# Attention and expert block: the first chunk's value products in key-tile order, with the wait for the fourth tile's copy moved ahead of its own products

## The reference, cut to what matters

```python
q, k, v = (einsum('bnd,fd->bnf', layernorm(x), W) for W in (Wq, Wk, Wv))   # heads of 64
sim = 50 * tanh(einsum('bhid,bhjd->bhij', q, k) * 64**-0.5 / 50)
attn = softmax(where(causal, sim, lowest))
x = x + einsum('bhij,bhjd->bhid', attn, v) @ Wo.T
x = x + shared_ffn(layernorm(x)) + top2_experts(layernorm(x))
```

## Time and profile before

| what | value |
|---|---|
| median of 3 runs | 2019.36 us (2017.86 to 2020.98) |
| profiled execution | 2022.81 us |
| its span from first to last instruction | 2021.0 us |
| TensorE matmul busy | 1915.1 us, 95% of the span |
| TensorE weight loads busy | 1496.6 us, 74% |
| VectorE busy | 1514.7 us, 75% |
| ScalarE busy | 1414.5 us, 70% |
| GpSimd busy | 1014.9 us, 50% |

### The profile page before, as it was taken

The page is one execution under the profiler, slowest core; times in us unless marked ns, Lnnn a source line. Parts: engine busy times, 40 slices in busy tenths (PEclk is TensorE's granted clock), DMA queues, the critical chain, the costliest instruction groups (busy, mean ns, idle before and its releaser), DMA issues. The chain is left out here.

```text
span 2021.0 us, 40088 instructions
## 1 busy us (share of the span) xinstructions
PE 1915.1 (95%) x14511; PEld 1496.6 (74%) x14511; DVE 1514.7 (75%) x2933; ACT 1414.5 (70%) x2169; POOL 1014.9 (50%) x1195
## 2 busy tenths in 40 slices
PE   6899999999999999999999999999999985998998
PEld 5676767676777777777777777777777754898998
DVE  5577777777878787878777777777777676677777
ACT  6878787878787777777777777777777752444444
POOL 4444555555555545454646464646454542444444
PEclk9999999999999999999999999999999996999999
DMA  4000000000000001010101010101010124665764
GB/s 136 1 12 10 32 22 32 22 33 22 27 27 22 32 17 38 12 43 12 43 12 43 12 43 12 43 12 43 11 43 1 43 74 152 211 189 175 207 196 132
DMA packets 74511, 113.56 MB, mean 56 GB/s; under 512 B 10441, under 2 KB 52942, under 8 KB 74192
## 3 DMA queue, kind: packets, MB, share of 16 engines
q1 hardware_dynamic: 59312, 68.90, 11.5%
q0 software_dynamic: 15008, 42.10, 5.5%
HBM read 64.13 MB, written 48.65 MB: 56 GB/s over the span
## 5 line engine op out<-in xcount | busy, mean ns | idle before, releaser
L523 POOL TENSOR_SCALAR_AFFINE_SELECT prob<-prob 128x256 f32<-128x256 f32 x512 | 222.7, 456 | 651.1 <-ACT prob L613 646.1
L607 ACT ACTIVATE prob<-ring 128x1024 f32<-128x1024 f32 (+1 forms) x384 | 324.1, 874 | 159.7 <-PE ring L1275 152.7
L613 ACT ACTIVATE prob<-prob 128x1024 f32<-128x1024 f32 (+1 forms) x384 | 346.6, 917 | 6.0
L808 DVE TENSOR_TENSOR kT<-ring,kT 64x512 fp32r<-64x512 f32 x256 | 176.3, 689 | 204.2 <-ACT kT L620 171.1
L1291 PE MATMUL bank_o<-prob,v 128*32 128x512 f32 (+3 forms) x4096 | 302.5, 435 | 18.1 <-issue 15.4
L535 POOL TENSOR_TENSOR key_sum<-prob 128x768 f32<-128x768 f32 x128 | 239.4, 1870 | 85.0 <-PE bank_d L1306 68.5
L1291 PEld LDWEIGHTS bank_o<-prob,v 128*32 128x32 f32 x4096 | 116.8, 109 | 184.9 <-issue 174.0
L1270 PE MATMUL ring<-qT,kT 128*128 128x256 f32 (+3 forms) x1024 | 239.9, 336 | 12.4 <-ACT qT L630 8.6
L1270 PEld LDWEIGHTS ring<-qT,kT 128*128 128x128 f32 x1024 | 162.9, 189 | 88.5 <-issue 39.5
L822 DVE RECIPROCAL norm<-bank_d 128x512 f32<-128x512 f32 x64 | 214.7, 3354 | 17.9 <-PE bank_d L1306 17.3
L1275 PE MATMUL ring<-q_lo,kT 128*128 128x256 f32 (+3 forms) x1024 | 227.0, 323 | 0.0
(11 more groups left out here) (222 smaller groups left out, 4654.9 us busy)
## 6 DMA issues: line engine op xcount, KB each, us to landing
xin<-first SPq DMA_DIRECT2D x71, 257.0 KB
xin<-second SPq DMA_DIRECT2D x71, 129.0 KB
xin<-base SPq DMA_DIRECT2D x71, 128.0 KB
x_next<-in_x SPq DMA_DIRECT2D x16, 512.0 KB, 3.9
x_res<-in_x SPq DMA_DIRECT2D x16, 512.0 KB, 3.9
raw_e<-in_w SPq DMA_DIRECT2D x4, 1024.0 KB, 6.6
first<-pad SPq DMA_DIRECT2D x9, 257.0 KB, 6.9
second<-pad SPq DMA_DIRECT2D x9, 129.0 KB, 6.5
```

The costliest lines, as they stand in the source:

```text
L523: last = nc.gpsimd.affine_select(out=diag, in_=diag, compare_op=ALU.is_ge, fill=0.0, base=0, pattern=[[0, 2], [1, P]], channel_multiplier=-1)
L607: nc.scalar.activation(probs[p % PROBS][u][:, :, :], slot[:, :, 0:UNIT_COLS[u]], ACT.Tanh, scale=SCALE / SOFTCLAMP).then_inc(act_emptied, 1)
L613: nc.scalar.activation(cols, cols, ACT.Exp, scale=SOFTCLAMP).then_inc(exp_done, 1)
L808: last = nc.vector.tensor_tensor(kT[head_rows[1 - h], h, :], slot[r, 1, :], kT[r, h, :].bitcast(F32), ALU.subtract)
```

## The change

In `values` the list of key tiles is sorted by key tile (0, 1, 2, 3 in place of 0, 1, 3, 2), in all 128 chunks. In chunk 0 of a sequence the wait ahead of the products is for the copy of `v`'s tile 2 (`NT - 2`) in place of tile 3, and the wait for tile 3's copy stands just ahead of the products of key tile 3. The sum over key tiles is the same, taken in another order.

```diff
--- before.py
+++ after.py
@@ -1281,11 +1281,13 @@
                 g, quad, half = i * PAIRS + c, c // 2, c % 2
                 if g >= 1:
                     pe.wait_ge(o_steps, 3 * (g - 1) + 1)
-                units = [(u, j, at) for u in range(3) for j, at in SCORE_UNITS[u]]
+                units = sorted(((u, j, at) for u in range(3) for j, at in SCORE_UNITS[u]), key=lambda unit: unit[1])
                 if c == 0:
-                    pe.wait_ge(act_emptied, EMPTIED[AT["v", i, NT - 1, 0]][0])
+                    pe.wait_ge(act_emptied, EMPTIED[AT["v", i, NT - 2, 0]][0])
                 pe.wait_ge(masked, 3 * (i * PAIRS + 2 * quad + 1) + 3)
                 for k, (u, j, at) in enumerate(units):
+                    if c == 0 and j == NT - 1:
+                        pe.wait_ge(act_emptied, EMPTIED[AT["v", i, NT - 1, 0]][0])
                     for h in range(QUAD):
                         f = (quad * QUAD + h) * DH + half * QD
                         last = pe.matmul(bank_o[h * QD:(h + 1) * QD, j * P:N], v[:, j, f:f + QD],
```

## The result

The changed kernel takes 1999.26 us (median of 4 runs, 1996.17 to 2002.47) against 2018.76 for the kernel before (4 runs, the three shown and one more, 2017.86 to 2020.98). The ratio is 0.9897, 95% interval 0.9876 to 0.9917. Faster, as forecast, and by a little more: 17.8 us were forecast and 19.5 lie between the medians. The interval of the ratio gives 1994.3 to 2002.6 on the same scale, so this miss is smaller than the uncertainty of the measurement; but the gain lies nearer to the end of the range than to its middle, and the range was too narrow on that side.

A forecast was written before the change was run, and what follows sets the result against it. TensorE's chain was taken to bound the attention, so its idle time counts. 15 x 1.06 + 1.9 = 17.8 us, off the median of 2019.36, gave 2001.6 us, with a range of 1999.0 to 2008.

The forecast's parts named there:

- The wait and its share of the time: TensorE, chunk 0: idle 0.90 us in sequences 1 to 15 for ScalarE's copy of v's tile 3; 15 of 16 entries.
- Rival C: Chunk 0: nothing happens, another wait holds it or tile 3's products take the gap's place; 2019.4 us, chance 0.04.
- 1.06 for a sequence: Chunk 0 of sequences 1 to 15: values start directly behind the denominators, gaining 1.06 us each, bounds 0.90 and 1.10.
- Sequence 0: Chunk 0 there: three tiles run before the copy ends, a break of about 0.9 stays; gain 1.9 us, lower bound 0.9.
- The order at nothing: All 128 chunks: 128 columns standing last in place of 256 cost 0; bounds 1.3 us either way.
- the met wait at nothing: Chunk 0, ahead of key tile 3: the new wait is met with 0.97 us to spare, costs 0; upper bound 0.8 us.
- Rival A: Chunk 0: the values' first load of 0.11 us stands exposed behind the denominators' last pass; 2003.3 us, chance 0.05.
- Rival B: At p = 3 or 4, VectorE's reciprocal and GpSimd's DMAs set the pace, half the lead goes; 2009.5 us, chance 0.06.
- make L788 late by 0.7: VectorE's L788 waits for GpSimd's DMAs, landing some 0.7 us late; hidden by VectorE's 0.92 us idle.
- The range: Whole kernel: 1999.0 to 2008 us, with rival A inside and rivals B and C outside.
- Best end: Low end of the range: 18.4 us plus 0.5 of the order, off the lowest run of 2017.86, gives 1999.0 us.

The follow-up runs named there:

- e3: From the kernel before: key tile order stays 0, 1, 3, 2, only the wait moves to just ahead of tile 3; ratio 0.9900.
- e6: From the kernel before, TensorE unchanged: ScalarE copies v's tile 3 ahead of pair 2's unit 1 exponential (sequence 0: ahead of the w_o cast); ratio 0.9915.
- e2: From the kernel before: key tiles in their order in all chunks, all waits still ahead of the products; ratio 0.9999.
- e5: From the changed kernel: chunk 0's tile 3 products read v's tile 2, and the wait for tile 3's copy stands ahead of chunk 1; stretch 1514.07 us.
- e7: From the changed kernel: in sequence 0 ScalarE copies v's tile 3 ahead of the w_o cast; ratio 0.9891 to the kernel before.
- e1: The changed kernel once more, with more timings, against the kernel before; ratio 0.9893.
- e10: The kernel before measured against itself; ratio 1.0005.
- e9: The changed kernel a third time, against the kernel before; ratio 0.9899.

## Why the prediction was right or wrong

*The wait and its share of the time: right.* The idle time called "issue" was the wait for ScalarE's copy; moving only the wait (e3) brings 17.9 us, and moving the copy (e6) 13.6. Rival C, that nothing happens, is out by the same runs.

*1.06 for a sequence: right in mechanism, short by 3%.* The period fell from 102.40 to 101.30, by 1.10. From the last denominator product to the first value product it is now 0.30, where the prediction took 0.33; and from the chunk's first product to the scores it is 2.267 in place of 2.291, where the prediction had "still 2.29". That last gain belongs to the moved wait: e3 with the old order has 2.267, e2 with the new order 2.291. The two together are 1.10 to 1.11, and 0.01 at most is given back.

*Sequence 0: right.* 5.76 - 3.82 = 1.94 against 1.9, with the break of 0.7 to 0.9 where it was put.

*The order at nothing, the met wait at nothing: right*, by e2 and by e5 against e7. One reading behind it is loose: 973.33 - 973.09 = 0.24 is called the streaming time of two 128-column passes, which the prediction takes as 0.22 in sequence 0.

*Rival A, the load that stands bare: wrong.* The values' first weights load at 961.93, while products of the denominators, with weights in the same 128 rows, are in flight (the group of L1308 from 961.61 for 0.83), and the products start without a further step. This is against the sentence of the Trainium skill ("TensorE: Matmul & The Clock Gate", Part 3, The mechanism) that such a load overlaps "only when row_grp differs"; the trace decides.

*Rival B, the lead is lost at p = 3 or 4: wrong here.* VectorE kept 1.11 (1.17 forecast), and the period shows that 0.01 at most is lost. Nor did the DMAs make L788 late by 0.7, as the prediction feared: it starts 12.09 behind the chunk's first product (974.35 - 962.26), and 12.12 before (987.18 - 975.06). The last of the four was issued at 971.20 and L788 ran at 974.35, so it had landed within 3.15 us; the 3.9 of the earlier trace rows was of a load of another kind.

*The range: wrong.* The step that failed is "Best end: 15 x 1.10 + 1.9 = 18.4 with 0.5 of the order, off the lowest run". Its sizes of the mechanism hold: the stretch lost 18.3 us. What it put at nothing, without a row for it, is everything outside the 16 first chunks ("the gain is in the attention"), where the first two profiles lost another 8.3 us: 1.0 ahead of the stretch, 1.5 in the last chunks, 5.7 behind them. The same program varies there: it took the spread of three runs of the kernel before (3.1 us) for that of both kernels, while the changed kernel's own four runs spread by 6.3, the kernel before by 8.9 in the 17 runs beside e1, and the expert stage of the changed kernel by 11 us in three profiles. A few us below the sum belonged in the range, where it had 2.6 below and 6.4 above. The claim that the tail wait of chunk 7 (1.9 us) is "one that the change does not touch" holds for the code, but its time did change: in the three profiles of the changed kernel chunk 7 starts 66.4 to 67.7 after chunk 0 of sequence 15, in the first one of before 70.1.

*What stays open.* Three measurements of the changed kernel give 0.9893 to 0.9899, or 20.4 to 21.6 us; the stretch explains 18.3 to 18.7. The 2 to 3 us between lie outside the stretch, within each single interval but on the same side three times. The part from chunk 0 of sequence 15 to the experts has the right size for them (2.2 less in the first pair, 1.2 from e2 to e1, 4.1 from e10 to e9). That the change causes this is not shown.

## What to carry to other kernels

When an engine stands still ahead of a group of products, ask which of its operands is late and put the wait ahead of that one alone; a wait that the list calls "issue" finds its name in the timeline, by what ends 0.1 us before the start. Read the price from start to start, not from the idle column (1.10 against 0.90), and check that the engines whose work is anchored to an earlier event (here VectorE's reciprocal and GpSimd's DMAs) have more idle time than the lead you create. Before setting a range, find the stages of the kernel that scatter without being changed, and add their scatter for both kernels. Compare the granted clock of those stages as well, stage by stage and not only in the 40 slices of the page.

## What the runs showed of the hardware that wasn't expected

- A stage bound by TensorE with matmuls repeats within 0.3 us in 1500 on three chips, while the expert stage of the same kernel differs by 8 to 11 us, together with 0 to 11 stops of ScalarE of about 2 us that have no releaser on the core. One of three chips had none in its four profiles.
- Weight loads of 32 columns over all 128 rows (0.11 us) run under matmuls that use the same rows, with no step: the next group starts 0.30 us behind the last of four 384-column passes, and passes of that width stand 0.32 apart.
- A met semaphore wait between matmuls costs nothing that can be seen: 1514.17 us with 16 of them in the middle of chunk 0, 1514.07 with them at the head of chunk 1.
- Within the stretch the granted clock stays at its upper level in all thirteen profiles; behind it the time at the lower level differs from profile to profile. The same products of the shared part took 8.09 us at 0.65 and 5.53 at 1.00.
- The end of a group of 128x32 products costs the same whether 128 or 256 columns stand last: 1533.81 against 1533.85 us over 121 chunks.
